# Attention products with V for two heads at a time, with a V projection between the pairs

## The reference

```python
q = apply_rope((query @ wq).reshape(bs, sq, HQ, DK).transpose(0, 2, 1, 3), pos)
k = apply_rope(repeat(key @ wk), arange(sk))
v = repeat(value @ wv)                      # each K/V head serves 4 query heads
attn = softmax(q @ k.T / sqrt(DK) + mask)   # 128 x 2048 a head
out = (attn @ v).transpose(0, 2, 1, 3).reshape(bs, sq, HQ * DV) @ wo
```

## Time and profile before

| | before |
|---|---|
| median of 3 runs | 695.34 us |
| profiled execution, its own time | 697.47 us |
| span of the profiled execution | 695.7 us |
| TensorE busy | 656.4 us, 94% |
| VectorE busy | 584.2 us, 84% |
| ScalarE busy | 444.6 us, 64% |
| POOL busy | 341.1 us, 49% |
| mean granted TensorE clock | 0.983 |

### The profile page before, as it was taken

The page is one execution under the profiler, slowest core; times in us unless marked ns, Lnnn a source line. Parts: engine busy times, 40 slices in busy tenths (PEclk is TensorE's granted clock), DMA queues, the critical chain, the costliest instruction groups (busy, mean ns, idle before and its releaser), DMA issues.

```text
span 695.7 us, 11704 instructions
## 1 busy us (share of the span) xinstructions
PE 656.4 (94%) x3615; PEld 557.8 (80%) x3615; DVE 584.2 (84%) x1186; ACT 444.6 (64%) x633; POOL 341.1 (49%) x187
## 2 busy tenths in 40 slices
PE   8999799899989989989988998999999999999997
PEld 7888578678867867867877886799988898989886
DVE  5999579869949978976985996977998899999996
ACT  4475469368466756936937756573877667676772
POOL 2355223722714333362272252300399887888783
PEclk9999899999989999999999999999999999999999
DMA  8719614913931871691392194682649988888620
GB/s 313 280 32 219 174 60 122 216 58 104 230 114 60 198 194 60 151 241 54 89 225 85 65 237 120 242 336 98 227 158 387 375 333 308 325 302 331 242 120 17
DMA packets 137781, 130.47 MB, mean 188 GB/s; under 512 B 119200, under 2 KB 120352, under 8 KB 128032
## 3 DMA queue, kind: packets, MB, share of 16 engines
q1 hardware_dynamic: 137760, 130.21, 60.7%
HBM read 100.51 MB, written 0.33 MB: 145 GB/s over the span
## 4 chain that ended last, share of the span: by engine, by line
PE 64%; DMA 16%; SPq 8%; POOL 4%; DVE 4%; issue 2%; ACT 1%; POOLq 0%; DVEq 0%
PE bank L458 17%; PE bank L460 15%; PE bank L459 15%; DMA halves<-halves 10%; PE bank L705 9%; SPq L346 6%; DMA halves<-high 5%; PE bank L817 3%; POOL w_out_lo L1748 2%; SPq L340 2%; POOL w_gate_lo L1753 1%; DMA wqo_raw<-in_wq 1%; PE bank L560 1%; DVE halves L1241 1%; PE bank L610 1%
## 5 line engine op out<-in xcount | busy, mean ns | idle before, releaser
L1688 POOL TENSOR_TENSOR k_lo<-rope_a,k_hi 128x512 fp32r<-128x512 f32 x32 | 51.8, 1627 | 111.0 <-ACT k_hi L891 111.0
L1356 DVE CAST pt_lo<-halves 128x512 fp32r<-128x512 f16 x112 | 49.4, 446 | 45.8 <-PE bank L460 33.2
L458 PE MATMUL bank<-pt_hi,v_hi 128*128 128x512 f32 (+1 forms) x144 | 59.2, 411 | 25.2 <-DVE pt_lo L1356 13.4
L1274 DVE CUSTOM_DVE_ANT_0 probs<-bank,mask_sb 128x512 f32<-128x512 f32 x128 | 82.0, 685 | 0.0
L921 ACT ACTIVATE pt_hi<-halves 128x512 fp32r<-128x512 f16 x112 | 67.6, 628 | 18.4 <-PE bank L460 11.7
L1748 POOL TENSOR_TENSOR w_out_lo<-w_out_sb,w_out_hi 128x2048 fp32r<-128x2048 f32 x16 | 73.5, 4591 | 5.1 <-ACT w_out_hi L1094 5.1
L891 ACT ACTIVATE k_hi<-rope_a 128x512 fp32r<-128x512 f32 x32 | 20.1, 628 | 81.8 <-DVE rope_a L1216 81.8
L1753 POOL TENSOR_TENSOR w_gate_lo<-w_gate_sb,w_gate_hi 128x2048 fp32r<-128x2048 f32 x14 | 64.5, 4604 | 14.8 <-ACT w_gate_hi L1086 14.8
L1241 DVE SCALAR_TENSOR_TENSOR halves<-probs,high 128x2048 f16<-128x2048 f32 x28 | 70.7, 2562 | 0.1
L705 PE MATMUL bank<-xnT,w_hs_sb 128*128 128x128 f32 x512 | 60.6, 277 | 0.0
L1725 POOL TENSOR_TENSOR wqo_lo<-wqo_raw,wqo_hi 128x1024 fp32r<-128x1024 f32 x14 | 33.5, 2416 | 51.1 <-ACT wqo_hi L873 51.1
(11 more groups left out here) (228 smaller groups left out, 1844.6 us busy)
## 6 DMA issues: line engine op xcount, KB each, us to landing
w_hs_sb<-in_w_hs SPq DMA_DIRECT2D x16, 1024.0 KB, 4.9
w_out_sb<-in_w_out SPq DMA_DIRECT2D x16, 1024.0 KB, 6.4
w_gate_sb<-in_w_gate SPq DMA_DIRECT2D x16, 1024.0 KB, 4.9
wqo_raw<-in_wq SPq DMA_DIRECT2D x8, 1024.0 KB, 4.8
mask_sb<-in_mask SPq DMA_DIRECT2D x8, 1024.0 KB, 4.8
wqo_raw<-in_wo SPq DMA_DIRECT2D x8, 1024.0 KB, 6.2
decay<-decay_rows SPq DMA_DIRECT2D x16, 512.0 KB, 6.9
ctx_raw<-in_ctx_t SPq DMA_DIRECT2D x3, 1024.0 KB, 10.9
```

What stands on the lines that cost most here:

```text
L458: pe.matmul(dst, left_hi, right_hi, start=first, stop=False)
L1274: dve.tensor_tensor_reduce(out=probs[:, h, b * 512:(b + 1) * 512], in0=ring_a[b][:, :], in1=mask_sb[:, b * 512:(b + 1) * 512], scale=1.0, ...
```

## The change

The steps of the loop are regrouped by head pairs. There are still 16 steps: eight for heads 0 and 1, eight for heads 2 and 3. A step takes two key tiles of 128 for two heads, so its parts are again 128 x 512, and TensorE makes six matmuls of 256 columns in it. Pair 0 adds into `pv_bank`, pair 1 into `oq_bank`, which the reciprocal row sums must have left. The casts of a pair wait only for that pair's high halves (`turned_high[pair]`). The fourth V block of the next group, which stood ahead of all steps, now stands between the pairs. The transposes of the next first V block move from step 6 to step 10, and with them `v_high` and `v_low`. `attn_hi` and `attn_lo` are made by pair; those of pair 0 stand within the steps of pair 1 on ScalarE and VectorE. Their place in memory moves to the start of the probabilities' buffer.

```diff
-VALUE_TURN = 6
+VALUE_TURN = 10
...
-        sb("probs_of_three", [P, HG - 1, SK], F32, output)
...
+        out_pair_bank = [pv_bank, oq_bank]
...
+        turned_high = [whole.enter_context(nc.semaphore(f"turned_high{i}")) for i in range(2)]
...
-                    .then_inc(s["turned_high"], 16)
+                    .then_inc(turned_high[h // 2], 16)
...
+            def values(g, u):
+
+                pair, step = u // HALF_STEPS, u % HALF_STEPS
+                pe.wait_ge(s["pt_hi_ready"], KT * g + u + 1)
+                pe.wait_ge(s["pt_lo_ready"], KT * g + u + 1)
+                for j in range(2):
+                    tile, cols = 2 * step + j, HALVES[j]
+                    last = pairs(out_pair_bank[pair][:, 0:DM // 2], v_hi[:, tile, :], v_lo[:, tile, :],
+                                 pt_hi[u % 3][:, cols], pt_lo[u % 3][:, cols], tile == 0, tile == KT - 1)
+                last.then_inc(s["pv_step"], 1)
+
             def attend(g):
                 project_v_block(g + 1, 1)
                 project_v_block(g + 1, 2)
-                project_v_block(g + 1, 3)
-                for t in range(KT):
-                    pe.wait_ge(s["pt_hi_ready"], KT * g + t + 1)
-                    pe.wait_ge(s["pt_lo_ready"], KT * g + t + 1)
-                    pairs(pv_bank[:, :], v_hi[:, t, :], v_lo[:, t, :], pt_hi[t % 3], pt_lo[t % 3], t == 0, t == KT - 1)\
-                        .then_inc(s["pv_step"], 1)
-                    if t == VALUE_TURN:
+                for u in range(KT):
+                    if u == HALF_STEPS:
+                        pe.wait_ge(s["inverse_ready"], g + 1)
+                        project_v_block(g + 1, 3)
+                    values(g, u)
+                    if u == VALUE_TURN:
                         transpose_v_block(g + 1, 0)
...
-            def attn_high(g):
-                act.wait_ge(s["pv_step"], KT * (g + 1))
-                act.activation(attn_hi[:, :, :].rearrange("p h t -> p (h t)"), pv_bank[:, :], ACT.Copy)\
-                    .then_inc(s["attn_hi_ready"], 1)
+            def attn_high(g, pair):
+                act.wait_ge(s["pv_step"], KT * g + HALF_STEPS * (pair + 1))
+                act.activation(attn_hi[:, 2 * pair:2 * pair + 2, :].rearrange("p h t -> p (h t)"),
+                               out_pair_bank[pair][:, 0:DM // 2], ACT.Copy).then_inc(s["attn_hi_ready"], 1)
...
+                    if step == 0:
+                        act.wait_ge(turned_high[pair], 32 * (g + 1))
+                    if u == 2:
                         act.wait_ge(s["k_lo_ready"], KB * (g + 2))
...
+                    act.activation(pt_hi[u % 3].rearrange("p (t h q) -> p t h q", t=2, h=2),
+                                   halves[:, 2 * pair:2 * pair + 2, 0, 2 * step * P:2 * (step + 1) * P]
+                                   .rearrange("p h (t q) -> p t h q", t=2), ACT.Copy).then_inc(s["pt_hi_ready"], 1)
...
+                    if u == HALF_STEPS + 2:
+                        attn_high(g, 0)
+                    if u == VALUE_TURN + 2:
+                        v_high(g + 1, 0)
```

More of the change, by code:

```diff
@@ L282, in build @@
             qT_lo_ready vproj_ready v_copied vT_mm v_hi_ready v_lo_ready scores_ready scores_masked neg_max_ready
-            probs_ready high_half_ready low_half_ready turned_high pv_step pT_mm pt_hi_ready pt_lo_ready pv_ready inv_sum_ready inv_hi_ready inv_lo_ready diag_ready
+            probs_ready high_half_ready low_half_ready pv_step pT_mm pt_hi_ready pt_lo_ready pv_ready inv_sum_ready inv_hi_ready inv_lo_ready diag_ready
             bcast_mm bcast_ready attn_out_ready oproj_ready xres_ready small_in dequant_in gate_in0 gate_in1
@@ L346, in turn_high @@
                 sp.dma_start_transpose(halves[:, h, 0, :].rearrange("p (t q) -> p t q", q=P), high_half[h])\
-                    .then_inc(s["turned_high"], 16)
+                    .then_inc(turned_high[h // 2], 16)
             def reload_mask(g):
-                sp.wait_ge(s["turned_high"], 16 * HG * (g + 1))
+                sp.wait_ge(turned_high[1], 32 * (g + 1))
                 sp.dma_start(mask_sb[:, :], mask).then_inc(s["mask_in"], 16)
@@ L913, in turned_high_parts @@
             def turned_high_parts(g):
[L914 to L917, removed]
-                        act.wait_ge(s["k_lo_ready"], KB * (g + 2))
[L919 to L925, removed]
+                for u in range(KT):
+                    pair, step = u // HALF_STEPS, u % HALF_STEPS
+                    if step == 0:
+                        act.wait_ge(turned_high[pair], 32 * (g + 1))
+                    if u == 2:
+                        act.wait_ge(s["k_lo_ready"], KB * (g + 2))
+                    if u >= 3:
+                        act.wait_ge(s["pv_step"], KT * g + u - 2)
+                    act.activation(pt_hi[u % 3].rearrange("p (t h q) -> p t h q", t=2, h=2),
+                                   halves[:, 2 * pair:2 * pair + 2, 0, 2 * step * P:2 * (step + 1) * P]
+                                   .rearrange("p h (t q) -> p t h q", t=2), ACT.Copy).then_inc(s["pt_hi_ready"], 1)
+                    if u == SUM_STEPS[1]:
                         act.wait_ge(s["inv_sum_ready"], g + 1)
@@ L949, in v_rest @@
                     if b == 0:
-                        attn_high(g - 1)
+                        attn_high(g - 1, 1)
                     else:
@@ L1335, in last_attn_low @@
                 two = slice(2 * pair, 2 * pair + 2)
-                dve.wait_ge(s["attn_hi_ready"], G + pair)
+                dve.wait_ge(s["attn_hi_ready"], 2 * (G - 1) + pair + 1)
                 dve.tensor_tensor(attn_lo[:, two, :].rearrange("p h t -> p (h t)"),
@@ L1348, in turned_low_parts @@
             def turned_low_parts(g):
[L1349 to L1358, removed]
+                for u in range(KT):
+                    pair, step = u // HALF_STEPS, u % HALF_STEPS
+                    if step == 0:
+                        dve.wait_ge(turned_high[pair], 32 * (g + 1))
+                    if u >= 3:
+                        dve.wait_ge(s["pv_step"], KT * g + u - 2)
+                    dve.tensor_copy(pt_lo[u % 3].rearrange("p (t h q) -> p t h q", t=2, h=2),
+                                    halves[:, 2 * pair:2 * pair + 2, 1, 2 * step * P:2 * (step + 1) * P]
+                                    .rearrange("p h (t q) -> p t h q", t=2)).then_inc(s["pt_lo_ready"], 1)
+                    if u == SUM_STEPS[0]:
                         inverse_sums(g)
-                    if t == VALUE_TURN + 4:
+                    if u == HALF_STEPS + 4:
+                        attn_low(g, 0)
+                    if u == VALUE_TURN + 4:
                         v_low(g + 1, 0)
@@ L1378, in add_head, with attn_low @@
                                          ALU.add).then_inc(s["xres_ready"], 1)
[L1380 to L1386, removed]
+            def attn_low(g, pair):
+                two = slice(2 * pair, 2 * pair + 2)
+                dve.wait_ge(s["attn_hi_ready"], 2 * g + pair + 1)
+                dve.tensor_tensor(attn_lo[:, two, :].rearrange("p h t -> p (h t)"), out_pair_bank[pair][:, 0:DM // 2],
+                                  attn_hi[:, two, :].rearrange("p h t -> p (h t)").bitcast(F32), ALU.subtract)\
+                    .then_inc(s["attn_lo_ready"], 1)
             dve.wait_ge(s["xres_ready"], 16)
@@ L1432, in _ @@
                 turned_low_parts(g)
-                attn_low(g)
+                attn_low(g, 1)
                 v_low(g + 1, 1)
```

## The result

The changed kernel takes 714.89 us (median of 4 runs, 712.63 to 716.86), the kernel before 696.46 us (4 runs, 694.68 to 698.07). The ratio is 1.0264, 95% interval 1.0221 to 1.0307. The prediction was 716, range 706 to 722. The profiled execution of the changed kernel is the fastest of its four (712.63 us, span 710.9), and that of before, 697.47 us, lies near the slow end of its runs (the slowest took 698.07), so the two spans differ by 15.2 us where the medians differ by 18.4.

A forecast was written before the change was run, and what follows sets the result against it. TensorE, busy 94%, was taken to wait mainly on VectorE's and ScalarE's lists. Six iterations at +2.2 (13.2), the first +0.6 and clock +6.6 gave +20.4 on 695.3, so 716 us, range 706 to 722.

The forecast's parts named there:

- The two layers of the wait: TensorE's 3.41 us wait before products with V: about 0.7 transposes of heads 2 and 3, 2.7 VectorE's and ScalarE's lists.
- Pair 0 starts earlier: First products with V no longer wait for heads 2 and 3: gain 0.7 us in six iterations, 2.3 in the first.
- The block on the path: Fourth V block, moved behind pair 0, loses the wait that covered it: cost 2.7 us per iteration, bounds 0 and 5.4.
- Narrow products: 48 matmuls of 512 columns with V become 96 of 256: cost 0.4 us per iteration, bounds 0 and 0.9.
- The end of the iteration: Around the output projection and next first mask, only a shorter attn_hi counts: gain 0.2 us per iteration, bounds 0 and 0.6.
- VectorE's list: VectorE's work ahead of the first part, first mask to last K rotation: stays as it is, still 36 us.
- Clock: TensorE's granted clock in the seven value stretches, lower after longer idle: 16.8 us lost, 6.6 more than before.
- (1): Rival: TensorE never idles, pair 0 starting when the third V block ends; 661 us, 3%, with 1% for smaller gains.
- (2): Rival: the fourth V block is covered because pair 1 waits for its parts from slow ScalarE; 697 us, 5%.
- (3): Rival: TensorE's clock gets no worse, losing 10.2 us as before, 709 us; 699 if it loses nothing; 22% together.
- (4): Rival: TensorE's clock stays low further, into the fourth V block, 7 x 1.4 us more; 726 us, 7%.

The follow-up runs named there:

- e6: Kernel before, without pairs, with the last K block's rotation moved from VectorE's list ahead of the first parts into the steps; 695.54 us, ratio 0.9982.
- e4: e1 with the last K block's rotation moved behind steps 2, 4, 6 and 8, dependent ScalarE work later; 663.18 us, ratio 0.9513 to the kernel before.
- e5: Changed kernel with 20 additional 512-column matmuls, results unused, behind the third V block to fill TensorE's wait; 700.07 us, ratio 1.0043 to the kernel before.
- e1: Changed kernel with the fourth V block put back ahead of pair 0, all else kept; 692.13 us, ratio 0.9937 to the kernel before.
- e2: Kernel before with only the fourth V block moved, behind the eighth of the sixteen four-head steps; 721.51 us, ratio 1.0347.
- e7: Kernel before with 12 additional 512-column matmuls, results unused, behind the fourth V block to fill TensorE's wait; 688.16 us, ratio 0.9884.
- e3: e4 with the fourth V block between the pairs again, as in the changed kernel; 679.47 us, ratio 0.9763 to the kernel before.

## Why the prediction was right, point by point

- **The two layers of the wait.** Right. 0.7 us was the transposes (e6 shows them as the bound once the lists are shorter), the rest the lists (e4).
- **Pair 0 starts earlier.** Predicted 0.7 us in six iterations and 2.3 in the first, 6.5 in all. The waits went from 25.2 to 37.6 us though a block of 2.73 left the front: 7 x 2.73 - 12.4 = 6.7.
- **The block on the path.** Predicted 2.7. Filled, the stretch takes 14.87 with the block (e5) and 12.13 without (e1 at clock 1.00): 2.74. No part of it is covered.
- **Narrow products.** Predicted 0.4, measured 0.53.
- **The end of the iteration.** Predicted 0.2. From the last product's end (212.00) to the next first mask it is now 5.65 us; before, 5.89 (209.01 in the trace to 214.90).
- **VectorE's list.** I costed it as unchanged. In the third iteration it is 35.48 instead of 35.85 us, 0.37 shorter: the second low half used to wait 0.12 us for ScalarE and now does not, and the masks wait less too. The first iteration does not have this; over the other six it is about 2.3 us that the sum did not have. It comes with the pairs: e1 has it too (35.51 us), e2 has not (35.83).
- **Clock.** In the profile the term that was furthest off. Predicted: 16.8 us lost, 6.6 more than the 10.2 of before. Measured in the profile: 12.9, so 2.7 more. The stretches lose 1.2 to 2.5 us after waits of 5.3 to 5.4, where I had taken 2.4 for each from a single row. In the fifth iteration, and likewise in the seventh, the clock was at 0.50 already while TensorE waited. It costs nothing there, and these two stretches lose 1.5 us. A stretch of the fifth wait, with no matmul in it:

```profile
311.70:315.00 3.30, 0.00 (x0) 0.00 (x0) 2.64 (x7) 1.67 (x4) 0.96 (x1) 0.50 0.91 195
```

The medians lose more: 14.8 by e5, and before 696.78 - 688.16 = 8.6 by e7, or 10.2 with what its first stretch still lost. That is 4.6 to 6.2 more, so the profiled execution was a mild one.

The sum with the measured terms: 7 x (2.74 + 0.53) = 22.9 for block and narrow products, + 2.7 clock, - 6.7 for the earlier start, - 2.3 list, - 7 x 0.24 = 1.7 at the end: 14.9, against 15.2 between the spans.

In the medians the forecast was +20.4 us and the change +18.4. That 716 and 714.9 lie 1.1 us apart is partly luck: the forecast stood on a median of 695.34, which became 696.46 with the fourth run, and the list, which it lacked, was taken back in part by the narrow products (7 x 0.13 = 0.9).

The rivals fell: TensorE does idle (1), pair 1 waits for nothing (2), the clock did get worse by a few us (3), and it did not stay low into the block (4): in the sixth iteration, which lost most, it is 1.00 from 380.00 on, and the block starts at 382.56.

## What to carry to other kernels

Before work is moved out of a wait to fill another, ask what ends the wait: here the visible releaser was a DMA, but two engines' own instruction lists ended only 0.7 us before it, and no transfer and no division by pairs could shorten them. Where a wait has two layers, taking away one moves the bound to the other; here only both together paid (5%, against 0.6% and 0%). And the independent block was worth most ahead of the longest wait, not between two pieces of work that were both ready.

## What was not expected of the hardware

Short waits cost TensorE's clock too. After 2.7 us idle, five of e1's seven stretches ran partly at the low level, up to 2.7 us longer; after about 1.15 and 0.47 us, two of e3's seven, by 1.5 us; after 0.6 to 0.9 us (e5, and e7 but for its first) none. The longest loss hardly changed with the wait: 2.7 us after 2.7 (e1), 2.6 after 3.4 (before), 2.5 after 5.4 (the changed kernel).

And VectorE's cast of a part, 0.43 us, took longer when it began while POOL's k_lo was running: in all 61 such casts of the traces it ended 0.28 to 0.29 us after that k_lo, whatever it took (0.50 to 1.51 us). In e3 two casts in a row, beside two k_lo, took 0.90 and 1.50 us and ended at 183.60, the k_lo at 183.31:

```profile
181.28 2.32 DVE L1390 CAST pt_lo<-halves 128x512 fp32r<-128x512 f16 x2
...
180.16 3.15 POOL L1725 TENSOR_TENSOR k_lo<-rope_a,k_hi 128x512 fp32r<-128x512 f32 x2
```

In the changed kernel the third cast began 0.07 us before a k_lo, at 194.63, and took 0.41 us.
